# Causal attention with a dealt-out maximum pass: the second half of group 0 or the first half of group 1 as second phase

## What is computed

```python
q = jnp.einsum('btc,hcd->bhtd', x, Wq) + bq[None, :, None, :]      # k and v alike
scores = jnp.einsum('bhtd,bhsd->bhts', q, k) * scale
probs = jax.nn.softmax(scores + causal, axis=-1)
y = jnp.einsum('bhts,bhsd->bhtd', probs, v)
return y.transpose(0, 2, 1, 3).reshape(Bn, Tn, H * D) @ Wo + bo
...
x = x + _layernorm(_L0_attn_ref(_layernorm(x), ...))                # then the experts, then both again
```

## Time and profile before

| | |
|---|---|
| median of 3 runs | 754.69 us (753.72 to 756.21) |
| profiled execution, its own time | 756.23 us |
| span of its trace, first to last instruction | 754.5 us |
| L0: first maximum reduced to the start of step 28 | 34.5 to 125.3 us |
| L1: the same | 435.0 to 526.4 us |

### The profile page before, as it was taken

How to read it: one execution, slowest core, us unless ns; L and a number is a source line. 1 busy time by engine, 2 the same in 40 slices (tenths; PEclk the granted TensorE clock), 3 DMA queues, 4 the chain that set the end, 5 groups by cost and what they waited for, 6 DMA issues and landing times.

```text
span 754.5 us, 13333 instructions
## 1 busy us (share of the span) xinstructions
PE 671.9 (89%) x4388; PEld 441.6 (59%) x4388; DVE 477.3 (63%) x1264; ACT 322.4 (43%) x680; POOL 262.9 (35%) x308
## 2 busy tenths in 40 slices
PE   3988999999668999999975888999998899999991
PEld 2633444435447999999963533444444456999970
DVE  4588788864582444444475788788865785343457
ACT  2554666673133333222242533666664231433322
POOL 4140112111156676444431183112211203677621
PEclk9999999999679999999996979999999999999995
DMA  3534210070018999999770345002000630489762
GB/s 101 144 124 140 64 36 2 1 231 23 28 51 298 301 323 313 313 312 311 263 244 0 107 125 161 16 16 104 2 1 2 205 98 18 144 285 313 236 204 97
DMA packets 60294, 108.60 MB, mean 144 GB/s; under 512 B 11194, under 2 KB 37131, under 8 KB 60100
## 3 DMA queue, kind: packets, MB, share of 16 engines
q1 hardware_dynamic: 52532, 93.86, 37.9%
q0 software_dynamic: 7632, 13.86, 5.7%
q10 hardware_dynamic: 64, 0.03, 0.0%
HBM read 79.98 MB, written 19.79 MB: 132 GB/s over the span
## 4 chain that ended last, share of the span: by engine, by line
PE 71%; DVE 20%; DMA 3%; issue 2%; ACT 2%; POOL 1%; SPq 1%; ACTq 0%; DVEq 0%; POOLq 0%
PE ps L1156 17%; PE ps L983 9%; PE ps L901 8%; PE ps L969 7%; DVE mx L1622 6%; PE ps L1169 5%; PE ps L1171 5%; PE ps L1015 4%; PE ps L1095 3%; PE ps L853 3%; PE ps L1127 2%; DVE X L2014 2%; PE ps L904 2%; PE ps L934 1%; DMA outs<-X,token 1%
## 5 line engine op out<-in xcount | busy, mean ns | idle before, releaser
L1622 DVE TENSOR_REDUCE mx<-ps 128x1 f32<-128x512 f32 (+3 forms) x304 | 184.6, 656 | 37.8 <-PE ps L904 18.3
L1324 ACT ACTIVATE X<-ps 128x1024 f32<-128x1024 f32 (+1 forms) x192 | 147.5, 809 | 84.7 <-PE ps L969 84.4
L901 PE MATMUL ps<-KA,QA 112*128 112x512 bf16 (+3 forms) x384 | 118.4, 345 | 7.4 <-DVE mx L1622 3.3
L780 POOL DMA_INDIRECT outs<-X,token x95 | 94.9, 999 | 77.0 <-DVE X L1994 61.9
L748 POOL TENSOR_SCALAR_AFFINE_SELECT X<-X 128x512 f32<-128x512 f32 x64 | 40.7, 637 | 208.3 <-ACT X L1324 208.3
L1156 PE MATMUL ps<-QA,KA 128*128 x756 | 95.9, 277 | 2.6 <-issue 2.2
L969 PE MATMUL ps<-QA,KA 114*128 114x512 bf16 (+3 forms) x384 | 95.0, 330 | 2.6 <-ACT X L1324 1.2
L1981 DVE TENSOR_TENSOR X<-ps,X 128x128 f32<-128x128 f32 x95 | 27.7, 291 | 108.2 <-ACT X L1441 108.0
L1156 PEld LDWEIGHTS ps<-QA,KA 128*128 128x128 f32 x756 | 93.0, 193 | 4.8 <-issue 3.0
L901 PEld LDWEIGHTS ps<-KA,QA 112*128 112x128 bf16 x384 | 37.7, 100 | 85.2 <-DVE mx L1622 54.8
L772 POOL DMA_INDIRECT V<-token_rows,row_of_slot x64 | 65.6, 1025 | 57.1 <-DVE row_of_slot L1895 31.5
(11 more groups left out here) (304 smaller groups left out, 869.2 us busy)
## 6 DMA issues: line engine op xcount, KB each, us to landing
KA<-in_ex SPq DMA_DIRECT2D x95, 512.0 KB
X<-in_dn SPq DMA_DIRECT2D x95, 64.0 KB
outs<-empty SPq DMA_DIRECT2D x4, 1024.0 KB, 8.5
V<-outs SPq DMA_DIRECT2D x4, 1024.0 KB, 7.9
QA<-X SPq DMA_DIRECT2D x28, 128.0 KB, 2.5
KA<-X SPq DMA_DIRECT2D x28, 128.0 KB, 2.5
QA<-w_sdn SPq DMA_DIRECT2D x28, 128.0 KB, 2.5
KA<-parts_k SPq DMA_DIRECT2D x28, 128.0 KB, 2.4
```

The source lines that it names most:

```text
L780: pool.indirect_dma_start(out=outs[L], out_offset=bass.IndirectOffsetOnAxis(ap=token[L][:, i:i + 1], axis=0), in_=erows[:, g % OUT_RING, : ...
L901: mm = pe.matmul(ps[:, bank, j * w:(j + 1) * w], QA[0:KQ, h, i * P:(i + 1) * P], KA[0:KQ, h, s0:s0 + w], start=True, stop=not diag)
L1324: nc.scalar.activation(probs[:, st % PB, 2 * p:2 * p + 2, off:CH], ps[:, 4 + 2 * p:6 + 2 * p, off:CH], ACT.Exp, scale=SCALE).then_inc(S(f" ...
L1622: v.tensor_reduce(mx[:, part, i, h0:h0 + nh], ps[:, n % RB, 0:nh * w].rearrange("p (h w) -> p h w", h=nh), AX.X, ALU.max)\
```

## The change

```diff
-PHASES = ((0, 0), (0, 1), (1, 0), (1, 1), (2, 0), (3, 0), (2, 1), (3, 1))
+PHASES = ((0, 0), (1, 0), (0, 1), (2, 0), (1, 1), (3, 0), (2, 1), (3, 1))
...
-OWN_AHEAD = 6
-LATE_K = {4: (6, 0), 7: (6, 1), 10: (7, 0), 13: (7, 1)}
-DEALT = ((((0, 1),), 0, 4), (((1, 0),), 3, 4), (((1, 1),), 4, 13), (((2, 0), (3, 0), (2, 1)), 13, 29), (((3, 1),), 29, 37))
-ROWS_BEHIND = ((0, 1),)
-ROWS_AT = {(1, 0): 5, (1, 1): 13, (2, 0): 18, (3, 0): 21, (2, 1): 29, (3, 1): 37}
-ROWS_BY_ACT = 2
+AHEAD = ((1, 0), 6)
+LATE_K = {3: (6, 0), 5: (6, 1), 7: (7, 0), 9: (7, 1)}
+DEALT = ((((1, 0),), 0, 2), (((0, 1),), 2, 6), (((2, 0),), 6, 9), (((1, 1),), 9, 17), (((3, 0),), 17, 21), (((2, 1),), 21, 29),
+         (((3, 1),), 29, 37))
+ROWS_BEHIND = ((1, 0), (0, 1))
+ROWS_AT = {(2, 0): 10, (1, 1): 17, (3, 0): 22, (2, 1): 29, (3, 1): 37}
+ROWS_BY_ACT = 3
...
-    out = maxima(0, 0) + [("rows", 0, 0)] + maxima(0, 1)[:OWN_AHEAD]
+    out = maxima(0, 0) + [("rows", 0, 0)] + maxima(*AHEAD[0])[:AHEAD[1]]
...
-                    if (g, c) == (1, 0):
+                    if n == ROWS_BY_ACT:
 
                         output_weights(L)
```

More of the change, by code:

```diff
@@ L165, in maxima @@
         return [("max", g, u) for u in range(CHUNK_UNITS[0] * c, CHUNK_UNITS[c])]
-    out = maxima(0, 0) + [("rows", 0, 0)] + maxima(0, 1)[:OWN_AHEAD]
+    out = maxima(0, 0) + [("rows", 0, 0)] + maxima(*AHEAD[0])[:AHEAD[1]]
     dealt = [[] for _ in range(NSTEP + HEAD_START)]
     for phases, first, last in DEALT:
-        units = [x for g, c in phases for x in maxima(g, c)[OWN_AHEAD if (g, c) == (0, 1) else 0:]]
+        units = [x for g, c in phases for x in maxima(g, c)[AHEAD[1] if (g, c) == AHEAD[0] else 0:]]
         for q, x in enumerate(units):
```

## The result

| | before | after |
|---|---|---|
| median | 754.21 us (753.50 to 756.21, 4 runs) | 764.7 us (761.85 to 765.91, 4 runs) |
| profiled execution, its own time | 756.23 us | 764.88 us |
| span of its trace | 754.5 us | 763.0 us |

The ratio is 1.0121, interval [1.0095, 1.0147]: slower by some 10 us. The forecast was 756.4, the end of the range 759.8. The profiled execution of before is 2.0 us above its kernel's median, that of after at its median, so these two traces show 8.5 of the medians' 10.5 us.

What follows compares the result with a forecast made beforehand. In the attention blocks DVE was taken as the limit before step 6, PE from there on. Terms gave L0 +1.4 and L1 +0.3, together +1.7 us on the median 754.69: 756.4 us, range 751.5 to 759.8.

Steps and rivals of the forecast that it cites:

- I therefore count no drop in the sum: PE's clock falling to 1.2 GHz behind pauses was given nothing in the sum and kept only as a rival.
- item 2: Turning r(1,0), now directly behind its last maximum, costs DVE 1.27 us in both blocks, like r(0,0).
- slower rival: Clock falls at turning r(0,1) before step 6, costing 1.7 us a block: 759.8 us, or 758.1 for one; chance 0.34.
- Item 7: In L1 POOL's masks of steps 0 and 1 come late; PE waits 0 to 0.6 us, taken as 0.2.
- Item 1: The 12th reduction waits for group 1's copies and starts later: +1.8 us in L0, +1.0 in L1.
- item 6: L0's fourth projection product moves ahead of r(0,0), which may come later: 0 to 0.9 us, taken as 0.2.
- Item 3: r(0,1) moves behind the first 49 maxima, removing its stop: 1.73 us in L0, 2.07 in L1.
- Item 4: The 49th maximum is done at 68.67 us in L0, 468.62 in L1; step 6 starts at 69.80 and 469.75.
- Items 5 and 8: Step 6 against old step 5, 0.68 us PE work ahead: L0 +0.9, L1 -0.2; uneven later units: 0.3 a block.
- Item 9: Queues: ACT's extra transfers, 1.20 us, delay nothing, at most 1.2; output weights and group 2's copies cost nothing.
- faster rival: Added stops coincide with existing ones, so the late copies and extra bare turning cost nothing: -3.7, 751.0 us; chance 0.20.
- last signpost: Prediction wrong as a whole if the time between step 6 and step 28 changes by more than 0.3 us.

Runs made afterwards that it cites:

- e2: Kernel before, with 32 matmuls of unused product put in front of its bare turning r(0,1): 752.77 us, ratio 0.9974.
- e1: Kernel after, with matmuls of unused product (28 and 32) keeping PE busy in front of turnings r(1,0) and r(0,1): 758.8 us, ratio 1.0051.
- e6: Kernel after, with one POOL split in L1 made to wait for the negation of (1,0) and put behind two masks: 760.93 us, ratio 1.0088.
- e5: Kernel before, with turning r(1,0) moved directly behind its last maximum instead of at the end of step 5: 759.38 us, ratio 1.0068.
- e9: Kernel before, with turning r(0,1) moved two maxima later so that DVE has work meanwhile: 750.09 us, ratio 0.9957.
- e3: Kernel after, with both turnings r(1,0) and r(0,1) moved two maxima and a weigh later: 753.12 us, ratio 0.9982.
- e4: Kernel after, with the six units behind r(0,0) again those of (0,1) and all of (1,0) in steps 0 and 1: 766.27 us, ratio 1.0141.
- e12: Kernel after, with only turning r(1,0) moved two maxima and a weigh later, r(0,1) left bare: 758.83 us, ratio 1.0082.
- e8: Kernel after, with 32 matmuls of unused product in front of turning r(0,1) alone, r(1,0) left bare: 759.46 us, ratio 1.0074.

## Why the prediction was wrong

It named the right place and, as a rival, the right mechanism. Its sum had the right sign, +1.7 us, and a sixth of the size. The step that failed first is "I therefore count no drop in the sum": a term put at nothing, which by the rows is worth 6.3 of the 9.1 us missing in the blocks. Two more terms failed with it: the price of the bare turning in item 2 (1.4 us over both blocks), and POOL's hold on DVE, which no item has (2.0 us).

Two stretches of L1 in the trace of before that the prediction did not show, at the turnings r(0,0), where the clock is at 0.50 from 440.8 to 447.6, and r(0,1):

```profile
440.00:445.00 5.00, 3.27 (x16) 1.43 (x17) 4.83 (x10) 1.34 (x2) 2.12 (x1) 0.58 0.29 86
...
461.30:464.60 3.30, 3.30 (x22) 2.17 (x20) 2.44 (x5) 0.54 (x1) 0.00 (x0) 0.50 0.62 191
```

1. **The clock.** The slower rival described what happened: the clock falls at the turning r(0,1), right before work at PE's pace. Its price, 1.7 us for a drop of 3.4 us, was near: 1.54 measured. Three things were off. Its chance: the argument against it was that PE is busier between the maxima. It was, 8.04 of 9.00 us in 60 to 69, but it stands still in the turning itself (0.40 of 1.30), and behind that the clock fell. The rows to read were those of the stop, not the five microseconds around it, and before had them. It has four bare turnings, r(0,0) and r(0,1) in two blocks, and a stretch at 0.50 begins in three of them or within 2 us behind; "the trace agrees in one stretch only" left out the two of L1, shown above. In the second DVE is busy 2.44 of 3.30 us: there the drop was not hidden altogether, as e2 found. Its places: r(1,0) is as bare, and its drop on step 2 cost DVE about 1 us a block more, since only two reductions lie between the turning and PE's scores and weigh (second stop 1.40 and 1.56, where e1 in both blocks and e6 in L1, without a drop, have 0.47). Its length: in L1 it lasted 6.8 us and cost 2.28. Together, from the rows: L0 0.43 (the wait for PE 1.54 instead of 1.11) + 0.93 + 1.54, L1 1.09 + 2.28: 6.3 us. Filling both turnings gave back 5.9, or 4.5 against the old order's own fill.

   The Trainium skill's rule that the prediction weighed (TensorE: Matmul & The Clock Gate, "A second HAM failure mode: psum-queue depth-cycling") pointed to a loss of clock, which came. But the many bank waits it speaks of brought none in 60 to 69 us of after (1.00); the drops that carry the loss stand at the turnings.

2. **Item 2, the bare turning.** Priced at 1.27 from r(0,0) of L0. At full clock and without POOL it is 1.50 and a second stop of 0.47 (e6), 1.70 in the old order (e5). r(0,0) was the wrong row to take: behind it PE has units at hand, behind r(1,0) a step's scores and a weigh come first. The stop of r(0,1), 1.73 us, was the nearer row. (In the old order r(1,0) stands six units behind its last maximum, not three.)

3. **What the prediction did not see: POOL.** Item 7 asked when POOL's masks come out, not what POOL's splits do to DVE. The negation of (1,0) now falls beside a split and a mask in L1 and a mask in L0: 1.44 + 0.56 - 0.34 = 1.66 us and 0.55 - 0.17 = 0.38 us.

4. **Items 1 and 6.** The 12th reduction comes 9.20 us behind the first in L0 (forecast 9.59) and 9.25 in L1 (8.95). In L0 item 6 is the larger half of the shift: the negation of (0,0) stands 41.79 - 34.45 = 7.34 us behind the first reduction in place of 41.03 - 34.51 = 6.52, +0.82 where 0.2 was taken, near the bound of 0.9. Item 1 adds 0.6 there, in place of 1.8, and 1.3 in L1. **Item 3** held: the old stop is gone, and e9 shows a stop there to be worth about its length. **Item 4** failed through items 2 and 3 of this list and the clock: step 6 stands 36.97 and 38.24 us behind the first reduction instead of 35.29 and 34.80. **Items 5 and 8** held: by them step 6 to step 28 should be 57.22 (step 5 to step 28 before) - 0.68 + 0.3 = 56.8 us, and without drops it is 56.57; the 2.80 us from step 28 to 29, where before has 2.37, are another 0.4 a block that no item has. **Item 9** held as far as these times reach: the same 56.57 us contain step 6's exponentials and group 2's units, and from step 29 to 47 L0 takes 46.02 us in both orders. **Item 7** was not needed: w0 comes only at 458.03, behind the masks.

5. **The sum.** Forecast +1.4 and +0.3 in the blocks, measured +4.7 and +6.1, so 9.1 are missing: the clock 6.3, POOL 2.0, the clean price of the turning (1.97 - 1.27) 0.7 in each block is 1.4, items 1, 6 and 7 together -0.5, which makes 9.2, and small terms of both signs. The faster rival, in which added stops fall together with others and cost nothing, is refuted by e5, where one more stop cost 1.7 us and more.

The prediction's last signpost, that step 6 to step 28 must not change, was badly put: by its own item 5 the new step 6 stands against the old step 5.

Interleaving itself shows no gain. With both turnings hidden (e3) it comes to step 29 1.1 and 0.8 us before the old kernel, but that one still has its bare r(0,1); against the old order with that turning hidden (e9) it is 0.3 and 1.2 us later, in L1 with a negation that waits 1.3 us for POOL, and the medians are 753.1 and 750.1, each against its own before 0.9982 [0.9955, 1.001] and 0.9957 [0.9939, 0.9975].

## What to carry to other kernels

Price a stop at what runs behind it: under a slower engine it costs its length, in front of work at PE's pace it may cost PE's clock as well, and one bare turning of 1.7 us cost a block 3.05 (e5). Before moving a step into the open, look for two or three pieces of the next work to put between its wait and its use; that was a few lines of the planner here and brought 4 us (e9), where the whole new order lost 10. And when a small operation moves in time, look at what POOL runs in the new place.

## What was not expected of the hardware

DVE waits for POOL. A negation of 128x16 elements that takes 0.17 us in every row of before took 1.44 (after), 1.34 (e4), 1.59 (e1) and 1.48 (e3), and in each of these its end follows that of POOL's running split of 2.1 us by 0.02 to 0.03 us; with the split elsewhere it took 0.17 (e6). Beside a mask of 0.63 us it took 0.55. Reductions beside such splits keep their length: in L1 of after, those inside the split from 461.19 to 463.31 take 0.68 us each, as those behind it do. The Trainium skill (SBUF — State Buffer, "Who interferes with whom") says that DVE and GpSimd (POOL here) share a pair of ports that one instruction holds to its end, that a tensor_scalar may enter the mode that wants it and an operation with two inputs in SBUF wants it too, and that a reduction never does. By that rule the first two kinds would wait and the third would not, and the traces agree.

The same stop was followed by a half clock in one block and not in the other (e5, e12). In the traces of all runs the bare turnings r(1,0) and r(0,1) occur 24 times, and in 18 of them a stretch at 0.50 begins in the stop or within 2 us behind it; of the 8 filled ones (e1, e2, e8) none has one. So these drops are no fixed price of an order but a risk that it takes.
